# Feed-forward down products by tokens, bias and x1 added ahead on GpSimd, last attention chunk by tokens, end reordered

## Chip, cores and metric

The kernel runs on one core of one Trainium2 chip. The metric is device time in microseconds (us), the median of several executions; lower is better.

## The reference

One transformer layer with post-normalisation, batch 4, 1024 tokens, width 128, all in fp32. First a linear attention of 16 heads of 64:

```python
q, k, v = split(x @ W_qkv)                       # per head
q, k = relu(q @ W_f + b_f), relu(k @ W_f + b_f)
out = (q @ (k.T @ v)) / (q @ k.sum(tokens) + 1e-6)
x1 = layernorm(x + out @ W_out + b_out)
h = gelu(butterfly(x1 @ W_exp + b_exp, up_weights) + up_bias)   # 512 wide, exact gelu
y = butterfly(h, down_weights) @ W_con + b_con + down_bias
out = layernorm(x1 + y)
```

Both butterflies are linear, so the kernel folds each into one matrix, `wup` (128 x 512) and `wdn` (512 x 128), once at the start.

## The kernel before

Tokens are worked in 8 chunks of 512 (`n` = 0 to 7, `LAST` is 7). A hand-written schedule of 43 slots (`for s in range(SLOTS)`) is walked by TensorE (PE), ScalarE (ACT), VectorE (DVE) and GpSimd (POOL), each in its own program; tables such as `UPS`, `DOWN_SLOT` and `YT_SLOT` say in which slot a chunk's step stands, and semaphores join the engines. Every engine takes its instructions strictly in the written order. The keys' slots come first (0 to 27), then only queries, attention and feed-forward, then an end outside the slot loop for the last chunk, in two halves of 256 tokens (`g` = 0, 1).

One chunk goes so: DVE multiplies the queries by the reciprocals (`normalise_q`, L1179, tile `qn`), 8 pairs of heads a chunk; for the first three batches ACT and DVE split the product into a high and a low part (`qn_h`, `qn_l`), and PE adds three fast products per pair; in the last batch PE adds one plain fp32 product per pair (L686). The sum stands in bank `attn_ps` with features on the partitions. ACT copies it with the bias `b_out` into `attnT` (tile `late`), PE transposes it into the bank `desk` (L571), DVE adds x (`add_x`, L1204), takes statistics, GpSimd makes the reciprocal deviation (`rstd_of`, L522 and L525), and DVE normalises (`layer_norm_end`, L1197) to x1. PE transposes x1 into `desk`, ACT and DVE split it (`x1T_h`, `x1T_l`), PE makes four up products of three matmuls each into the three `ring` banks, ACT applies gelu into `hid` (L964).

`down(n)` (L732) then multiplies with `wdn` as stationary operand and `hid` as moving one, four matmuls of 128x512 that leave the result by features in a ring bank. `yT_copy` (ACT, L971) adds the bias into `yT` (tile `late`), `transpose_y` (PE, L571) turns it into `desk`, and `residual` (DVE, L1213) adds x1, followed by the second normalisation and the store. `desk` is one bank that many transposes share: each waits until its previous content has been taken (`take_desk`).

A plain fp32 matmul shows in the trace as two records, an fp32 transpose as one.

Of the kernel before, what the change touches and what calls it, by code (L numbers as in the profile page):

```python
# [5 lines left out]
def postln_linear_attention_butterfly_ffn_kernel(  # L6
# [106 lines left out]
    YT_SLOT = {}  # L113
    for n in range(ALLCH - 4):
        at = ATTN_LAST[n] + 3
        for i in range(HT):
            UPS[at + i] = [HT * n + i]
        DOWN_SLOT[at + HT] = n
        YT_SLOT[at + HT + 1] = n


    for n, ups, down, back in [(4, [33, 34, 35, 35], 36, 37), (5, [37, 37, 38, 38], 39, 42),
                               (6, [41, 41, 42, 42], None, None)]:
        for i in range(HT):
            UPS.setdefault(ups[i], []).append(HT * n + i)
        if n < LAST - 1:
            DOWN_SLOT[down] = n
            YT_SLOT[back] = n
# [13 lines left out]
    for s in range(SLOTS):  # L142
# [10 lines left out]
        if s in DOWN_SLOT:  # L153
            order.append(("down", DOWN_SLOT[s]))
# [3 lines left out]
    for use in [("down", LAST - 1), *[("up", HT * LAST + i, g) for g in range(2) for i in range(HT)],  # L158
                ("down", LAST, 0), ("down", LAST, 1)]:
        ring_of[use] = len(ring_of)  # L160
# [5 lines left out]
    for s in range(SLOTS):  # L166
# [5 lines left out]
        if s in YT_SLOT:  # L172
            order.append(("y", YT_SLOT[s]))
# [13 lines left out]
    for use in [("attn", LAST, 0), ("x1", LAST, 0), ("y", LAST - 1), ("y", LAST, 0)]:  # L187
        desk_of[use] = len(desk_of)
    spare_of = {("attn", LAST, 1): 0, ("x1", LAST, 1): 1, ("y", LAST, 1): 2}
# [5 lines left out]
    with ctx:  # L195
# [30 lines left out]
        bcon_col = sb("bcon_col", [128, 1])  # L226
        bdn_raw = sb("bdn_raw", [128, 1])
        bdn_col = sb("bdn_col", [128, 1])
# [24 lines left out]
        attnT, yT = late[:, 0, :], late[:, 1, :]  # L253
# [14 lines left out]
        coef_rows = sb("coef_rows", [HT, LOCAL, 256])  # L268
# [63 lines left out]
        s_smade = sem("spare_made")  # L332
        s_staken = sem("spare_taken")
# [34 lines left out]
        def half_bank(use):  # L368
            return desk if use[2] == 0 else spare_ps

        def half_made(use):

            return (s_dmade, desk_of[use] + 1) if use[2] == 0 else (s_smade, spare_of[use] + 1)

        def half_taken(use):
            return (s_dtaken, desk_of[use] + 1) if use[2] == 0 else (s_staken, spare_of[use] + 1)
# [4 lines left out]
        def _(sp):  # L381
# [47 lines left out]
            column(bcon_col[:, :], b_con)  # L429
            column(bdn_raw[:, :], down_bias)  # L430
# [40 lines left out]
            for n in range(1, LAST + 4):  # L471
                if n < ALLCH:
                    spread(n)
                if n >= 4:
                    store_out(n - 4)
# [8 lines left out]
        def _(pool):  # L484
# [34 lines left out]

            def rstd_of(i, n):  # L520
# [10 lines left out]
            for s in range(SLOTS):  # L531
                if s == WEIGHTS_SLOT:
                    pool.wait_ge(s_wuh, 1)
                    g.tensor_tensor(wup_l[:, :], y_up[:, :], wup_h[:, :].bitcast(fp32), ALU.subtract).then_inc(s_wul, 1)
                if s in ATT_T_SLOT:
                    rstd_of(0, ATT_T_SLOT[s])
                if s in YT_SLOT:
                    rstd_of(1, YT_SLOT[s])

# [11 lines left out]
            rstd_half(0, 1)  # L551
            rstd_of(1, LAST - 1)
# [4 lines left out]
        def _(pe):  # L557
# [117 lines left out]
            def add_attn(a):  # L675
# [6 lines left out]
                elif p == 0:  # L682
                    pe.wait_ge(s_atc, a // PAIRS)
                if a >= WHOLE:
# [24 lines left out]
            def transpose_y(n):  # L709
                take_desk(("y", n))  # L710
                pe.wait_ge(s_taken, ring_of["down", n] + 1)
                transpose_tiles(desk, lambda i: yT[:, i * 128:(i + 1) * 128]).then_inc(s_dmade, 1)

# [11 lines left out]

            def down(n):
                take_ring(("down", n))
                if n == 0:
                    pe.wait_ge(s_dtaken, desk_of["wdn",] + 1)
                for i in range(HT):  # L730
                    pe.wait_ge(s_taken, ring_of["up", HT * n + i] + 1)
                    last = t_.matmul(bank(("down", n))[:, :], wdn[:, i, :], hid[:, i, :],  # L732
                                     start=i == 0, stop=i == HT - 1)
                last.then_inc(s_made, 1)
# [27 lines left out]
            for s in range(SLOTS):  # L762
# [29 lines left out]
                if s in YT_SLOT:  # L792
                    transpose_y(YT_SLOT[s])
# [43 lines left out]
            def take_half(use):  # L837
                if use[2] == 0:
                    pe.wait_ge(s_dtaken, desk_of[use])
                elif spare_of[use]:  # L840
                    pe.wait_ge(s_staken, spare_of[use])
                else:

                    pe.wait_ge(s_dn, 3 * STAGES)

            def transpose_half(use, src):
                for i in range(2):
                    last = t_.transpose(half_bank(use)[:, i * 128:(i + 1) * 128], src(2 * use[2] + i), ident[:, :])
                last.then_inc(half_made(use)[0], 1)

            for g in range(2):
                take_half(("attn", LAST, g))
                pe.wait_ge(s_atc, LAST + 1 + g)
                transpose_half(("attn", LAST, g), lambda i: attnT[:, i * 128:(i + 1) * 128])
            down(LAST - 1)
            for g in range(2):
                take_half(("x1", LAST, g))
                pe.wait_ge(s_x1, LAST + 1 + g)
                transpose_half(("x1", LAST, g), lambda i: x1[:, LAST % X1BUF, i, :])
            for g in range(2):  # L860
# [9 lines left out]
                if g == 0:  # L870
                    transpose_y(LAST - 1)
            for g in range(2):
                use = ("down", LAST, g)
                take_ring(use)
                for i in range(HT):
                    pe.wait_ge(s_taken, ring_of["up", HT * LAST + i, g] + 1)
                    last = t_.matmul(bank(use)[:, 0:HALF], wdn[:, i, :], hid[:, i, g * HALF:(g + 1) * HALF],
                                     start=i == 0, stop=i == HT - 1)
                last.then_inc(s_made, 1)
            for g in range(2):  # L880
                take_half(("y", LAST, g))
                pe.wait_ge(s_taken, ring_of["down", LAST, g] + 1)
                transpose_half(("y", LAST, g), lambda i: yT[:, i * 128:(i + 1) * 128])

        @block.scalar
        def _(act):
# [72 lines left out]
            def gelu(f):  # L959
                n, i = f // HT, f % HT  # L960
                act.wait_ge(s_made, ring_of["up", f] + 1)
                if i == 0 and n:
                    act.wait_ge(s_made, ring_of["down", n - 1] + 1)
                a_.activation(hid[:, i, :], bank(("up", f))[:, :], ACT.Gelu, bias=bup_col[:, i:i + 1])\  # L964
                    .then_inc(s_taken, 1)

            def yT_copy(n):
                act.wait_ge(s_made, ring_of["down", n] + 1)
                if n:
                    act.wait_ge(s_dmade, desk_of["y", n - 1] + 1)  # L970
                a_.activation(yT[:, :], bank(("down", n))[:, :], ACT.Identity, bias=bdn_col[:, :]).then_inc(s_taken, 1)  # L971
# [18 lines left out]
            for s in range(SLOTS):  # L990
# [35 lines left out]
                if s in DOWN_SLOT:  # L1026
                    if s == min(DOWN_SLOT):
                        act.wait_ge(s_bc, 2)
                    yT_copy(DOWN_SLOT[s])
                for f in UPS.get(s, []):  # L1030
                    if f == 0:
                        act.wait_ge(s_bc, 2)
# [9 lines left out]
                if s == 5:  # L1042
                    act.wait_ge(s_bias, 16 * (3 + HT))
# [7 lines left out]
            act.wait_ge(s_at, PAIRS * ALLCH)  # L1051
            act.wait_ge(s_dmade, desk_of["attn", LAST - 1] + 1)
            for tok in halves:
                a_.activation(attnT[:, tok], attn_ps[:, tok], ACT.Identity, bias=bout_col[:, :]).then_inc(s_atc, 1)
            yT_copy(LAST - 1)
# [4 lines left out]
            act.wait_ge(s_made, ring_of["down", LAST - 1] + 1)  # L1060
            for g, tok in enumerate(halves):
                for i in range(HT):
# [4 lines left out]
            act.wait_ge(s_dmade, desk_of["y", LAST - 1] + 1)  # L1067
            for g, tok in enumerate(halves):
                use = ("down", LAST, g)
                act.wait_ge(s_made, ring_of[use] + 1)  # L1070
                a_.activation(yT[:, tok], bank(use)[:, 0:HALF], ACT.Identity, bias=bdn_col[:, :]).then_inc(s_taken, 1)

        @block.vector
        def _(dve):
# [126 lines left out]
            def add_x(n):  # L1201
                b, c = n // CHUNKS, n % CHUNKS
                dve.wait_ge(s_dmade, desk_of["attn", n] + 1)
                v.tensor_tensor(x1[:, n % X1BUF, :, :], desk[:, :].rearrange("p (t c) -> p t c", t=QUADS),  # L1204
# [4 lines left out]
            def residual(n):  # L1209
                dve.wait_ge(s_dmade, desk_of["y", n] + 1)  # L1210
                if n >= 2:
                    dve.wait_ge(s_out[n % 2], 16 * (n // 2))
                v.tensor_tensor(y[:, n % 2, :, :], desk[:, :].rearrange("p (t c) -> p t c", t=QUADS),  # L1213
                                x1[:, n % X1BUF, :, :], ALU.add).then_inc(s_dtaken, 1)
                dve.wait_ge(s_dtaken, desk_of["y", n] + 1)
# [29 lines left out]
            for s in range(SLOTS):  # L1245
# [30 lines left out]
                if s in YT_SLOT:  # L1276
                    residual(YT_SLOT[s])
# [7 lines left out]
                if s in YT_SLOT:  # L1285
                    layer_norm_end(1, YT_SLOT[s], y[:, YT_SLOT[s] % 2, :, :], s_yo)
# [18 lines left out]
                if s == WEIGHTS_SLOT:  # L1305
                    dve.wait_ge(s_bias, 16 * (3 + HT))
# [71 lines left out]
```

## Time and profile before

| | |
|---|---|
| median of 3 executions | 343.5 us (341.99 to 343.79) |
| the profiled execution, its own time | 344.24 us |
| its span in the trace | 342.4 us |
| PE busy | 321.1 us, 94% of the span |
| DVE busy | 229.2 us, 67% |
| ACT busy | 166.2 us, 49% |
| GpSimd busy | 81.9 us, 24%, nearly all of it before 80 us |
| mean granted PE clock | 0.997 of full speed |

Busy time of PE is the union of overlapping records, so start-to-start distances tell more of its pace than the length of one record. What is not in the span, 344.24 less 342.4, is 1.84 us.

### The profile page before, as it was taken

To read this page: it belongs to the slowest core of one execution; us is meant where nothing else is said; L and a number is where in the kernel's file an instruction comes from. 1 tells how busy PE (TensorE), PEld (TensorE's weight loads), DVE (VectorE), ACT (ScalarE), POOL (GpSimd) and SP (SyncE) were. 2 spreads that over 40 slices of the span, in tenths; PEclk is the share of its full clock that TensorE was granted. 3 is DMA by queue.
4 is the path that set the end of the run, shared out by engine and by line. 5 is a ranking of instruction groups with operands and counts; after the bars stand their busy time and mean duration, and the time that the engine had idled before them with its cause. 6 is when DMAs were issued, how large, how long until landed. Compare 5 with 4: busy or idle time off the path is not lost.

```text
span 342.4 us, 5147 instructions
## 1 busy us (share of the span) xinstructions
PE 321.1 (94%) x1845; PEld 224.2 (65%) x1845; DVE 229.2 (67%) x476; ACT 166.2 (49%) x280; POOL 81.9 (24%) x81
## 2 busy tenths in 40 slices
PE   5799899999999999999999999999999798989882
PEld 5666567767776776677767677577777566554462
DVE  3458999868698586857623876458637827477555
ACT  3533245435466454565474546365656543341451
POOL 4079999940000010101000110011001101111122
PEclk9999999999999999999999999999999999999998
DMA  6983143827406400900090006600380073740002
GB/s 185 281 273 134 71 174 124 299 77 182 125 2 144 107 0 6 235 11 3 8 228 15 0 2 144 138 0 3 77 202 2 3 191 90 164 127 18 24 9 62
DMA packets 25618, 33.75 MB, mean 99 GB/s; under 512 B 4184, under 2 KB 14456, under 8 KB 25592
## 3 DMA queue, kind: packets, MB, share of 16 engines
q1 hardware_dynamic: 25432, 33.38, 36.4%
q8 instruction: 15, 0.25, 0.3%
q14 instruction: 11, 0.09, 0.1%
q10 hardware_dynamic: 160, 0.03, 0.0%
HBM read 31.04 MB, written 2.36 MB: 98 GB/s over the span
## 4 chain that ended last, share of the span: by engine, by line
PE 72%; DVE 13%; DMA 5%; issue 4%; SPq 3%; POOL 2%; ACT 1%; POOLq 0%; DVEq 0%; ACTq 0%
PE ring L562 25%; PE kx_ps L636 12%; PE attn_ps L562 7%; PE ring L732 6%; PE ring L656 4%; PE attn_ps L686 4%; PE ring L616 3%; PE desk L571 3%; DMA bf_col<-in_L_attn_b_f_dram 2%; DVE qn L1179 2%; DMA x<-_L_ffn_down_weights_dram 2%; PE desk L670 2%; PE desk L645 2%; SPq L445 1%; DVE late L1096 1%
## 5 line engine op out<-in xcount | busy, mean ns | idle before, releaser
L908 ACT ACTIVATE q<-ring,bf_col 128x512 f32<-128x512 f32 x64 | 43.8, 688 | 52.1 <-PE ring L562 51.6
L522 POOL TENSOR_TENSOR var_eps<-mean_var,ln_eps 128x4 f32<-128x4 f32 x14 | 7.0, 503 | 223.8 <-DVE mean_var L1192 223.8
L636 PE MATMUL kx_ps<-k,xs 128*128 128x512 f32 x128 | 60.1, 592 | 0.0
L901 ACT ACTIVATE k<-ring 128x512 f32<-128x512 f32 x64 | 38.3, 598 | 28.3 <-PE ring L616 27.9
L1179 DVE TENSOR_TENSOR qn<-q,recips 128x512 f32<-128x512 f32 x64 | 42.3, 699 | 4.3 <-DMA recips<-recip_rows 4.3
L1078 DVE TENSOR_TENSOR qn_l<-qn,qn_h 128x512 fp32r<-128x512 f32 x48 | 32.2, 680 | 16.9 <-ACT qn_h L894 16.6
L514 POOL TENSOR_TENSOR y<-hid,y_up 128x512 f32<-128x512 f32 x18 | 35.4, 1986 | 15.3 <-DMA hid<-in_L_ffn_up_weights_dram 14.3
L894 ACT ACTIVATE qn_h<-qn 128x512 fp32r<-128x512 f32 x48 | 29.6, 627 | 14.8 <-DVE qn L1179 14.8
L562 PE MATMUL ring<-xT_h,wq_h 128*128 128x512 f32 x64 | 35.7, 558 | 0.0
L636 PEld LDWEIGHTS kx_ps<-k,xs 128*128 128x128 f32 x128 | 24.0, 189 | 17.8 <-issue 15.3
L1151 DVE TENSOR_TENSOR k_total<-k_total,k 128x1024 f32<-128x1024 f32 x24 | 34.4, 1432 | 0.9 <-ACT k L901 0.7
L562 PE MATMUL ring<-wk_h,xT_h 128*128 128x512 f32 x64 | 29.0, 453 | 0.0
L732 PE MATMUL ring<-hid,wdn 128*128 128x512 f32 x56 | 25.4, 596 | 0.0
L616 PE MATMUL ring<-bf_rows,ones_r 128*128 128x512 f32 x64 | 25.1, 393 | 0.1
L562 PE MATMUL ring<-xT_h,wq_l 128*128 128x512 f32 x64 | 25.2, 394 | 0.0
L562 PE MATMUL ring<-wk_h,xT_l 128*128 128x512 f32 x64 | 25.2, 394 | 0.0
L562 PE MATMUL ring<-xT_l,wq_h 128*128 128x512 f32 x64 | 25.1, 392 | 0.0
L562 PE MATMUL ring<-wk_l,xT_h 128*128 128x512 f32 x64 | 25.1, 392 | 0.0
L964 ACT ACTIVATE hid<-ring,bup_col 128x512 f32<-128x512 f32 x28 | 19.2, 686 | 10.5 <-PE ring L562 10.3
L562 PE MATMUL attn_ps<-qn_h,m_h 128*128 128x512 f32 x48 | 19.9, 415 | 1.1 <-DVE qn_l L1078 1.1
L562 PE MATMUL attn_ps<-qn_l,m_h 128*128 128x512 f32 x48 | 19.0, 395 | 0.0
L562 PE MATMUL attn_ps<-qn_h,m_l 128*128 128x512 f32 x48 | 18.8, 393 | 0.0
(159 smaller groups left out, 553.5 us busy)
## 6 DMA issues: line engine op xcount, KB each, us to landing
recips<-recip_rows SPq DMA_DIRECT2D x64, 256.0 KB, 5.2
hid<-in_L_ffn_up_weights_dram SPq DMA_DIRECT2D x9, 512.0 KB, 3.8
x<-_L_ffn_down_weights_dram SPq DMA_DIRECT2D x9, 512.0 KB, 4.4
xs<-in_L_attn_x_dram SPq DMA_DIRECT2D x4, 512.0 KB, 6.2
out_dram<-y SPq DMA_DIRECT2D x7, 256.0 KB, 3.7
q<-in_L_attn_W_qkv_dram SPq DMA_DIRECT2D x2, 512.0 KB, 9.0
q<-in_L_attn_W_qkv_dram SPq DMA_DIRECT2D x2, 256.0 KB, 3.1
q<-in_L_attn_W_out_dram SPq DMA_DIRECT2D x2, 256.0 KB, 8.7
```

The costliest lines, as they stand in the source:

```text
L514: g.tensor_tensor(term_up[f].rearrange("p (hi j lo) -> p hi j lo", j=2, lo=lo), w[:, :, :, :, f], yv[:, :, f:f + 1, :].to_broadcast([128, ...
L562: last = t_.matmul(dst, lhsT, rhs, start=start and n == 0, stop=stop and n == len(pairs) - 1)
L616: t_.matmul(dst, ones_r[:, :], bf_rows[:, :], start=False, stop=True).then_inc(s_made, 1)
L636: t_.matmul(kx_ps[half], xs[b % XBUF][:, t, :], k[kt % KRING][:, half * CH:(half + 1) * CH], start=t == 0, stop=t == TILES - 1).then_inc(s ...
L732: last = t_.matmul(bank(("down", n))[:, :], wdn[:, i, :], hid[:, i, :], start=i == 0, stop=i == HT - 1)
L894: a_.activation(dst, src, ACT.Copy).then_inc(done, 1)
L901: a_.activation(k[kt % KRING][:, half * CH:(half + 1) * CH], bank(("k", kt, half))[:, :], ACT.Relu).then_inc(s_taken, 1)
L908: a_.activation(q[:, i % QRING, :], bank(("q", i))[:, :], ACT.Relu, bias=bf_col[:, :])\
L964: a_.activation(hid[:, i, :], bank(("up", f))[:, :], ACT.Gelu, bias=bup_col[:, i:i + 1])\
L1078: v.tensor_tensor(dst, src, high.bitcast(fp32), ALU.subtract).then_inc(done, 1)
L1151: v.tensor_tensor(k_total[:, :], k_total[:, :], k[kt % KRING][:, :], ALU.add).then_inc(s_ks, 1)
L1179: v.tensor_tensor(qn[:, a % NRING, :], q[:, a % QRING, :], recips[:, a % PAIRS // RC, a % RC, :], ALU.mult).then_inc(s_qn, 1)
```

## The change

The down product is turned round: `hid` becomes the stationary operand and `wdn` the moving one, sixteen matmuls of 128x128 in four groups of 128 tokens (`down_group`), straight into the bank `spare_ps`, by tokens. The ACT copy and PE's transposes of y go away, and DVE's `residual` reads `spare_ps` directly. What `residual` added before, x1, and the bias are added ahead by GpSimd into `y` (`with_bias`, one addition of 128x512 a chunk, right behind the normalisation of x1). The biases come as rows, broadcast over the partitions by three DMAs that SP issues behind `spread(1)`; the two DMAs that loaded them as columns go.

The last chunk's attention is also made by tokens, four 128x128 matmuls a pair, so its copy and transposes go; GpSimd adds `b_out` to the last chunk of x in place, in slot 30. Chunk 6's four up products all stand in slot 42, behind the last attention sum. The end outside the loop is written in another order, and chunk 6's down product is split into its four groups between the last chunk's steps.

```diff
-                               (6, [41, 41, 42, 42], None, None)]:
+                               (6, [42, 42, 42, 42], None, None)]:
...
+            def with_bias(n, tiles, done):
+                pool.wait_ge(s_x1, done)
+                pool.wait_ge(s_brow, 1)
+                if n >= 2:
+                    pool.wait_ge(s_out[n % 2], 16 * (n // 2))
+                bias = bdn_row.rearrange("p (o c) -> p o c", o=1).to_broadcast([128, tiles.stop - tiles.start, C])
+                g.tensor_tensor(y[:, n % 2, tiles, :], x1[:, n % X1BUF, tiles, :], bias, ALU.add).then_inc(s_pre, 1)
...
-                if s in YT_SLOT:
-                    rstd_of(1, YT_SLOT[s])
+                if s in Y_SLOT:
+                    rstd_of(1, Y_SLOT[s])
+                if s in X1T_SLOT:
+                    with_bias(X1T_SLOT[s], slice(0, QUADS), X1T_SLOT[s] + 1)
+                if s == NO_KEYS + 2:
+                    pool.wait_ge(s_kxt, 2 * TILES * BATCH)
+                    last = xs[(BATCH - 1) % XBUF][:, (CHUNKS - 1) * QUADS:CHUNKS * QUADS, :]
+                    g.tensor_tensor(last, last, bout_row.rearrange("p (o c) -> p o c", o=1)
+                                    .to_broadcast([128, QUADS, C]), ALU.add).then_inc(s_xb, 1)
...
+            for h in range(2):
+                with_bias(LAST, slice(2 * h, 2 * h + 2), LAST + 1 + h)
             rstd_of(1, LAST - 1)
...
+                if a >= BATCH * STEPS - PAIRS:
+                    pe.wait_ge(s_qn, a + 1)
+                    for i in range(QUADS):
+                        tok = slice(i * 128, (i + 1) * 128)
+                        last = t_.matmul(attn_ps[:, tok], qn[:, a % NRING, tok], m_whole[:, p, :],
+                                         start=p == 0 and i == 0, stop=p == PAIRS - 1 and i == QUADS - 1)
...
+            def down_group(n, i, dst):
+                for j in range(HT):
...
+                    last = t_.matmul(dst, hid[:, j, i * 128:(i + 1) * 128], wdn[:, j, :],
+                                     start=j == 0, stop=j == HT - 1)
...
+            transpose_x1_half(0)
+            take_down(LAST - 1)
+            down_before_last(0)
+            transpose_x1_half(1)
+            down_before_last(1)
+            up_half(0)
+            down_before_last(2)
+            down_before_last(3)
+            up_half(1)
...
             def residual(n):
-                dve.wait_ge(s_dmade, desk_of["y", n] + 1)
...
+                dve.wait_ge(s_pre, n + 1)
...
+            layer_norm_half_end(0, 0, last_x1, s_x1)
+            layer_norm_end(1, LAST - 2, y[:, (LAST - 2) % 2, :, :], s_yo)
+            layer_norm_half_end(0, 1, last_x1, s_x1)
```

On PE, from slot 40 to the first up product of the last chunk, before:

```order
L686 MATMUL attn_ps<-qn,k_total 128x512 x2
L562 MATMUL ring<-x1T_h,wup_h 128x512
...
L686 MATMUL attn_ps<-qn,k_total 128x512
L571 MATMUL desk<-ident,late 128x128 x4
L686 MATMUL attn_ps<-qn,k_total 128x512
...
L848 MATMUL desk<-ident,late 128x128 x2
L848 MATMUL spare_ps<-ident,late 128x128 x2
L732 MATMUL ring<-hid,wdn 128x512 x4
L848 MATMUL desk<-ident,x 128x128 x2
L848 MATMUL spare_ps<-ident,x 128x128 x2
L562 MATMUL ring<-x1T_h,wup_h 128x256
```

The same stretch of the changed kernel, where L717 is the attention by tokens and L764 `down_group`:

```order
L717 MATMUL attn_ps<-k_total,qn 128x128 x16
L589 MATMUL ring<-x1T_h,wup_h 128x512
...
L888 MATMUL desk<-ident,x 128x128 x2
L764 MATMUL spare_ps<-wdn,hid 128x128 x4
L888 MATMUL attn_ps<-ident,x 128x128 x2
L764 MATMUL spare_ps<-wdn,hid 128x128 x4
L589 MATMUL ring<-x1T_h,wup_h 128x256
```

The last four attention sums now stand together ahead of chunk 6's up products; the transposes of attention and y are gone, and two groups of chunk 6's down product stand between the x1 transposes, ahead of the first up product.

On GpSimd, slots 30 to 32 of the changed kernel (before, the four rows of `var_eps` and `rstd` stood here alone):

```order
L536 TENSOR_TENSOR var_eps<-mean_var,ln_eps 128x4
L539 TENSOR_TENSOR rstd<-var_eps,minus_half 128x4
L562 TENSOR_TENSOR xs<-xs,rows 128x512
L536 TENSOR_TENSOR var_eps<-mean_var,ln_eps 128x4
L539 TENSOR_TENSOR rstd<-var_eps,minus_half 128x4
L532 TENSOR_TENSOR y<-x,rows 128x512
```

Two additions of 128x512 have come in, one behind the deviations of y (chunk 2), one behind those of x1 (chunk 4).

On DVE, the last chunk's first normalisation in the changed kernel; before, L1197 of y stood ahead of both additions, and the two pairs of L1329 of x together behind them:

```order
L1236 TENSOR_TENSOR y<-spare_ps,y 128x512
...
L1336 TENSOR_TENSOR x<-attn_ps,xs 128x256
...
L1336 TENSOR_TENSOR x<-attn_ps,xs 128x256
...
L1348 TENSOR_SCALAR x<-x,mean_var,rstd 128x128 x2
L1216 TENSOR_SCALAR y<-y,mean_var,rstd 128x128 x4
L1348 TENSOR_SCALAR x<-x,mean_var,rstd 128x128 x2
```

The normalisation of chunk 5's y (L1216) now stands between the two halves of x1.

## Rows read from the trace of the kernel before

**Rows 1.** The page: busy time by engine, and the chain that ended last.

```profile
PE 321.1 (94%) x1845; PEld 224.2 (65%) x1845; DVE 229.2 (67%) x476; ACT 166.2 (49%) x280; POOL 81.9 (24%) x81
...
PE 72%; DVE 13%; DMA 5%; issue 4%; SPq 3%; POOL 2%; ACT 1%; POOLq 0%; DVEq 0%; ACTq 0%
```

**Rows 2.** Timeline at one down product (start, length, engine, line, operation).

```profile
294.74 3.60 PE L732 MATMUL ring<-hid,wdn 128*128 128x512 f32 x8
...
298.18 0.60 PE L571 MATMUL desk<-ident,x 128*128 128x128 f32 x4
...
298.61 1.02 PE L686 MATMUL attn_ps<-qn,k_total 128*128 128x512 f32 x2
```

**Rows 3.** Timeline of PE at the start: plain fp32 128x128 matmuls.

```profile
5.61 1.96 PE L589 MATMUL attn_ps<-wf_diag,q 128*128 128x128 f32 x8
7.37 1.91 PE L589 MATMUL spare_ps<-wf_diag,q 128*128 128x128 f32 x8
...
15.94 1.06 PE L589 MATMUL spare_ps<-wf_diag,q 128*128 128x128 f32 x8
16.83 1.45 PE L636 MATMUL kx_ps<-k,xs 128*128 128x512 f32 x3
```

**Rows 4.** Timelines of DVE and of POOL around 130 and 137 us.

```profile
129.65 1.29 DVE L1179 TENSOR_TENSOR qn<-q,recips 128x512 f32<-128x512 f32 x2
137.47 2.38 DVE L1179 TENSOR_TENSOR qn<-q,recips 128x512 f32<-128x512 f32 x2
...
137.71 1.59 POOL L534 TENSOR_TENSOR wup_l<-y_up,wup_h 128x512 fp32r<-128x512 f32 x1 [9.12 <-ACT wup_h L894]
```

**Rows 5.** Timelines of DVE and PE, 255 to 290 us; in brackets the wait before.

```profile
261.71 1.12 DVE L1197 TENSOR_SCALAR y<-y,mean_var,rstd 128x128 f32<-128x128 f32 x4 [1.18 <-POOL rstd L525]
262.75 1.29 DVE L1179 TENSOR_TENSOR qn<-q,recips 128x512 f32<-128x512 f32 x2
...
269.53 1.28 DVE L1179 TENSOR_TENSOR qn<-q,recips 128x512 f32<-128x512 f32 x2
...
272.37 0.47 PE L562 MATMUL attn_ps<-qn_h,m_h 128*128 128x512 f32 x1 [0.59 <-DVE qn_l L1078]
...
274.68 1.09 PE L670 MATMUL desk<-vo,kx 128*64 128x128 f32 x16 [0.67 <-DVE x1T_l L1078]
```

**Rows 6.** Timelines of PE at three other waits for DVE.

```profile
195.42 0.66 PE L571 MATMUL desk<-ident,late 128*128 128x128 f32 x4 [0.62 <-DVE xT_l L1078]
...
300.33 0.66 PE L571 MATMUL desk<-ident,late 128*128 128x128 f32 x4 [0.69 <-DVE x1T_l L1078]
...
306.66 1.10 PE L686 MATMUL attn_ps<-qn,k_total 128*128 128x512 f32 x2 [0.31 <-DVE qn L1179]
```

**Rows 7.** Timeline and chain of the end, from 315 us.

```profile
315.92 0.68 DVE L1179 TENSOR_TENSOR qn<-q,recips 128x512 f32<-128x512 f32 x1
...
318.92 1.02 PE L686 MATMUL attn_ps<-qn,k_total 128*128 128x512 f32 x2
...
323.57 0.42 DVE L1316 TENSOR_TENSOR x<-desk,xs 128x256 f32<-128x256 f32 x1
...
328.38 1.85 PE ring L562 x12
...
330.66 1.55 PE ring L562 x12
...
330.70 0.69 DVE L1213 TENSOR_TENSOR y<-desk,x 128x512 f32<-128x512 f32 x1 [1.58 <-PE desk L571]
...
334.12 1.12 DVE L1197 TENSOR_SCALAR y<-y,mean_var,rstd 128x128 f32<-128x128 f32 x4 [1.40 <-POOL rstd L525]
...
336.00 0.42 DVE L1316 TENSOR_TENSOR y<-desk,x 128x256 f32<-128x256 f32 x1 [0.77 <-PE desk L848]
...
337.15 0.39 DVE L1316 TENSOR_TENSOR y<-spare_ps,x 128x256 f32<-128x256 f32 x1
```

**Rows 8.** DMA issues: count, KB each, median us to landing.

```profile
out_dram<-y SPq DMA_DIRECT2D x7, 256.0 KB, 3.7
```

More of the change, by code:

```diff
@@ L127, in postln_linear_attention_butterfly_ffn_kernel @@
             DOWN_SLOT[down] = n
-            YT_SLOT[back] = n
+            Y_SLOT[back] = n
     WEIGHTS_SLOT = 16
@@ L157, in postln_linear_attention_butterfly_ffn_kernel @@
             ring_of[use] = len(ring_of)
-    for use in [("down", LAST - 1), *[("up", HT * LAST + i, g) for g in range(2) for i in range(HT)],
-                ("down", LAST, 0), ("down", LAST, 1)]:
+    for use in [("up", HT * LAST + i, g) for g in range(2) for i in range(HT)]:
         ring_of[use] = len(ring_of)
@@ L252, in postln_linear_attention_butterfly_ffn_kernel @@
         late = sb("late", [128, 2, CH])
-        attnT, yT = late[:, 0, :], late[:, 1, :]
+        attnT = late[:, 0, :]
         x1 = sb("x1", [128, X1BUF, QUADS, C])
@@ L267, in postln_linear_attention_butterfly_ffn_kernel @@
         bias_rows = sb("bias_rows", [HT, 128])
-        coef_rows = sb("coef_rows", [HT, LOCAL, 256])
+        rows = sb("rows", [128, LOCAL * 256])
+        coef_rows = rows[0:HT, :].rearrange("p (s n) -> p s n", s=LOCAL)
+        bout_row, bdn_row, bcon_row = (rows[:, i * C:(i + 1) * C] for i in range(3))
         coef_cols = sb("coef_cols", [128, STAGES - LOCAL, 2, 4])
@@ L473, in _ @@
                     spread(n)
+                if n == 1:
+                    sp.wait_ge(s_br, 3 * LOCAL)
+                    for dst, src in [(bout_row, b_out), (bdn_row, down_bias), (bcon_row, b_con)]:
+                        sp.dma_start(dst, src.rearrange("(o n) -> o n", o=1).to_broadcast([128, C])).then_inc(s_rows, 16)
                 if n >= 4:
@@ L724, in up_tile, with take_down @@
                       (x1T_h[:, :], x1T_l[:, :])).then_inc(s_made, 1)
-            def down(n):
[L727 to L734, printed above, removed]
+            def down_group(n, i, dst):
+                for j in range(HT):
+                    if i % 2 == 0:
+                        use = ("up", HT * n + j, i // 2) if n == LAST else ("up", HT * n + j)
+                        pe.wait_ge(s_taken, ring_of[use] + 1)
+                    last = t_.matmul(dst, hid[:, j, i * 128:(i + 1) * 128], wdn[:, j, :],
+                                     start=j == 0, stop=j == HT - 1)
+                return last
+            def take_down(n):
+                if n == 0:
+                    pe.wait_ge(s_dn, 3 * STAGES)
+                    pe.wait_ge(s_dtaken, desk_of["wdn",] + 1)
+                else:
+                    pe.wait_ge(s_dnt, n)
+            def down(n):
+                take_down(n)
+                for i in range(QUADS):
+                    last = down_group(n, i, spare_ps[:, i * 128:(i + 1) * 128])
+                last.then_inc(s_down, 1)
             def bias_columns():
@@ L835, in _, with transpose_x1_half, up_half @@
                     transpose_x1(X1T_SLOT[s])
[L837 to L846, printed above, removed]
+            def transpose_x1_half(g):
+                use = ("x1", LAST, g)
+                if g == 0:
+                    take_desk(use)
+                pe.wait_ge(s_x1, LAST + 1 + g)
                 for i in range(2):
-                    last = t_.transpose(half_bank(use)[:, i * 128:(i + 1) * 128], src(2 * use[2] + i), ident[:, :])
+                    last = t_.transpose(half_bank(use)[:, i * 128:(i + 1) * 128], x1[:, LAST % X1BUF, 2 * g + i, :],
+                                        ident[:, :])
                 last.then_inc(half_made(use)[0], 1)
[L851 to L860, printed above, removed]
+            def up_half(g):
                 for i in range(HT):
@@ L869, in _, with down_before_last @@
                           (x1T_h[:, tok], x1T_l[:, tok])).then_inc(s_made, 1)
-                if g == 0:
-                    transpose_y(LAST - 1)
-            for g in range(2):
[L873 to L883, printed above, removed]
+            def down_before_last(i):
+                down_group(LAST - 1, i, spare_ps[:, i * 128:(i + 1) * 128]).then_inc(s_dgrp, 1)
+            transpose_x1_half(0)
[7 more added lines that the diff above has]
+            up_half(1)
+            for g in range(2):
+                use = ("y", LAST, g)
+                pe.wait_ge(*half_taken(("x1", LAST, g)))
+                for i in range(2):
+                    last = down_group(LAST, 2 * g + i, half_bank(use)[:, i * 128:(i + 1) * 128])
+                last.then_inc(half_made(use)[0], 1)
         @block.scalar
@@ L962, in gelu @@
                 if i == 0 and n:
-                    act.wait_ge(s_made, ring_of["down", n - 1] + 1)
+                    act.wait_ge(s_down, n)
                 a_.activation(hid[:, i, :], bank(("up", f))[:, :], ACT.Gelu, bias=bup_col[:, i:i + 1])\
                     .then_inc(s_taken, 1)
[L967 to L971, printed above, removed]
             act.wait_ge(s_wT, 1)
@@ L1059, in _ @@
                 hi(x1T_h[:, tok], half_bank(("x1", LAST, g))[:, 0:HALF], s_x1h)
-            act.wait_ge(s_made, ring_of["down", LAST - 1] + 1)
             for g, tok in enumerate(halves):
+                act.wait_ge(s_dgrp, 2 * g + 2)
                 for i in range(HT):
@@ L1066, in _ @@
                         .then_inc(s_taken, 1)
[L1067 to L1071, printed above, removed]
         @block.vector
@@ L1275, in _ @@
                     add_x(ATT_T_SLOT[s])
-                if s in YT_SLOT:
-                    residual(YT_SLOT[s])
+                if s in Y_SLOT:
+                    residual(Y_SLOT[s])
                 for a in split_spreads(s)[1:]:
```

114 lines of the change are left out of this document (54 added, 60 removed).

## The prediction

> **What bounds the kernel now.** I read the page first: PE is busy for 94% of the span and makes up 72% of the chain that ended last, DVE 13% [rows 1]. So time that goes from PE's program counts, except where PE waits for another engine. The second view is PE's timeline, for its pace and its waits. The third is DVE's timeline over the stretches where PE waits for DVE: from 261 to 276 us DVE pauses only for GpSimd's deviations (the 1.18 in the row at 261.71), and PE waits for it, 0.59 and 0.67 us in the two rows shown [rows 5], and shorter cases stand at 195, 300 and 306 us [rows 6]. The last is the end from 316 us, where PE, DVE and GpSimd hand single steps to each other.
>
> **Down product, by tokens.** Before: eight records from 294.74 to 298.18, 3.44 us, 0.43 a record [rows 2]. After: sixteen matmuls, 32 records. The trace has plain fp32 matmuls of just this shape, each with its own stationary load. Eight of them take 16.83 - 15.94 = 0.89 us, 0.111 each; earlier, eight took 7.37 - 5.61 = 1.76 us, 0.22 each [rows 3]. I take 0.111, since it is from an already running PE, as every down product is; 0.22 is the other bound. So 32 x 0.111 = 3.56 us, 0.12 more per chunk, six times inside the slot loop: +0.7 us. The last chunk's eight attention sums go from 0.86 to 0.89 each: +0.2.
>
> **Transposes of y removed.** Four transposes cost 298.61 - 298.18 = 0.43 us of PE [rows 2] (a like group; y's have the same shape). Five stand in PE's stream before the end, chunks 0 to 4. Chunk 0's is followed by PE waiting 0.62 us for DVE at 195.42, which only grows: 0 gained. Chunk 2's opens the stretch where DVE is late: 0. Chunks 1 and 3 give 0.43 each. Chunk 4's waited another 0.69 us for `desk` at 300.33 [rows 6]; of the 1.12 us, I let the wait for DVE's `qn` at 306.66, which grows as PE comes earlier, take back a third: -0.75. Together -1.6 us. ACT's copies were hidden behind PE and are worth nothing by themselves.
>
> **GpSimd's additions.** Two DVE products of 128x512, both inputs in SBUF, take 1.29 us at 129.65, but 2.38 us at 137.47, when GpSimd's addition of 128x512 (1.59 us) runs beside them: +1.1 us [rows 4]. `with_bias` is such an addition, and starts just when DVE goes from normalising x1 to the same pair of products. So each costs DVE up to 1.1 us, with 0 as the lower bound. For chunks 0, 1, 2, 3 and 5 DVE then has idle time or PE is still behind: cover, so 0 (1.1 each if the cover is gone). For chunk 4 it meets the pair at 269.53, with PE already waiting for DVE behind it [rows 5]: +1.1. The addition to x in slot 30 starts as GpSimd ends the deviations, at 261.7, beside the normalisation at 261.71 and the pair at 262.75 [rows 5]. No row shows a normalisation beside such an addition. If it is spared, a third of the 1.6 us is left for the pair, 0.4; if not, 1.1; I take the middle, +0.7. For chunk 6 see the end.
>
> The Trainium skill (GPSIMD Engine Reference, Key points) says GpSimd shares its SBUF interfaces with VectorE, with contention for instructions "in a 2-port perf mode or with two SBUF inputs". The trace agrees on the second kind, by the 2.38 us; no row shows the first kind. By that rule the slot-30 addition would cost its full 1.1 and my sum would end 0.4 us later. The page's advice to give elementwise work to VectorE speaks against the change as well.
>
> **The middle together:** +0.7 + 0.2 - 1.6 + 1.1 + 0.7 = +1.1 us by 316 us. The up products now leave the ring a bank earlier, and SP's three broadcasts of rows fall into a stretch where SP waits; both 0.
>
> **The end**, on before's time scale. `with_bias` of chunk 6 delays DVE's last products, which had 0.4 us of slack, so the one at 315.92 ends at 317.3 in place of 316.6. The last attention sum no longer waits behind two up products and a transpose: it ends near 318.3, against 318.92 + 1.02 = 319.94. DVE needs no transpose of y: `residual(5)` runs 317.3 to 319.3 (2.0 us: the 334.12 + 1.12 - 330.70 = 4.54 of a whole normalisation less the normalising 1.12 and the wait 1.40) [rows 7]. The last chunk's x1 addition then starts at 319.35, against 323.57.
>
> What follows is two programs. DVE: half 0 and half 1 at 1.15 each (336.00 to 337.15) until 321.65; GpSimd first has chunk 5's deviations (1.4) and then half 0's (a pair of shorter operations, I estimate 1.0 from that 1.4) to 321.7; normalising half 0 takes 0.6 (half of 1.12), chunk 5 takes 1.12, half 1 takes 0.6: 324.1. PE from there: transposes 0.4, a down group 0.9, up half 1.6 (1.85 and 1.55 in the rows), two groups 1.8, up half 1.6, the last two halves 1.8 each: 334.0. DVE: `residual(6)` can start behind the fourth group, 324.1 + 0.4 + 0.9 + 1.6 + 1.8 = 328.8, plus 0.2 to see it, and takes 4.54 to 333.55; half 0 then 1.15, and half 1 starts at 334.75. DVE is the later by a little. Before, that addition started at 337.15 [rows 7]; all behind it is unchanged. The end gives 337.15 - 334.75 = -2.4 us.
>
> GpSimd's two `with_bias` halves of the last chunk wait for the store of chunk 5, which lands 3.7 us [rows 8] after 323.5, at 327.2; two operations of at most 0.8 (half of 1.59) end at 328.8, ahead of `rstd_of(1, 6)` at 331. That costs 0; behind them stand those deviations, and a store that lands 2 us late would delay the end by about that.
>
> **Sum:** +1.1 - 2.4 = -1.3 us: 344.24 - 1.3 = 342.9 for an execution like the profiled one, which lies 0.7 above the median of the runs. Against the median: 343.5 - 1.3 = 342.2 us.
>
> **Rivals.**
> - *The additions are absorbed* (faster). If GpSimd's slowing of DVE reaches PE nowhere, 1.1 + 0.7 go from the middle and 0.55 from the end: -3.65, 339.9 us. For it: DVE has idle time around most chunks. Against: the 2.38 us row, and PE's waits right behind the pair at 269.53.
> - *DVE's lost time reaches PE in most chunks* (slower). Eight additions at 1.1 are 8.8 us; my sum holds 2.35 of it. Once more than 1.3 us beyond that reaches PE, the kernel is slower. If half of the remaining 6.4 does: +1.9, 345.4 us. For it: DVE runs near PE's pace also at 185 to 196 us. Against: PE waits for DVE there only once, 0.62 us.
> - *Small matmuls run at 0.22 us a record.* 3.6 us more for each of six down products, and 0.9 for each of eight attention sums and some 7 us at the end: over 30 us, 375. For it: the rows at 5.61; against: those at 15.94.
> - *The end is not shorter, since DVE's chain replaces PE's*: -2.4 shrinks to 0 and the middle's +1.1 stays, 344.6 us. Against: the 4 us earlier start of the x1 addition follows from removed steps alone.
>
> **Chances.** Forecast 0.45 (its own range 341.0 to 343.5), absorbed 0.32, DVE reaching PE 0.12, small matmuls 0.03, end not shorter 0.08. The range to hold 8 in 10 goes from the absorbed case with a little below it, 339.4, to the end-not-shorter case, 344.7. A measurement tells about 0.5%, 1.7 us, from no change, so faster means below 341.8. A third of the forecast's share and nearly all of the absorbed case lie there: 0.45. Slower means above 345.2: the small matmuls and most of DVE's case, 0.13. The rest, 0.42, is within 0.5%.
>
> **What would show it.** Down records 0.11 us apart, a down product of 3.5 to 3.7 us; `with_bias` at 1.3 to 2.1 us with the DVE pair beside it at 2.3 to 2.4; PE's waits near 267 to 276 us grown by 1 to 2 us in total; the last chunk's x1 addition 3 to 4 us earlier relative to the end of DVE's last product; the last half's addition some 5.2 us before the span's end as now. The prediction is wrong if those waits did not grow, if new waits of PE for `qn_l` stand in the keys' slots, or if the down products take 5 us or more.

## The result, and the profile after

| | before | after |
|---|---|---|
| median | 343.64 us (4 runs beside it) | 355.08 us (354.17 to 356.53, 4 runs) |
| profiled execution, its span | 344.24, 342.4 us | 354.17, 352.3 us |
| mean granted PE clock | 0.997 | 0.981 |

The ratio is 1.034, with an interval of 1.030 to 1.038: 11.4 us slower, where 342.2 was forecast and 344.7 was the upper end of the range. The page of the changed kernel, busy time and chain (for [rows 1]):

```profile
PE 321.5 (91%) x2041; PEld 242.2 (69%) x2041; DVE 232.1 (66%) x475; ACT 159.4 (45%) x269; POOL 95.4 (27%) x92
...
PE 63%; DVE 13%; DMA 8%; issue 5%; SPq 5%; POOL 4%; ACT 1%; POOLq 0%; DVEq 0%; ACTq 0%
```

PE has no more to do than before (321.1), but its share of the chain fell from 72% to 63%, and DMA, SP's queue and GpSimd rose from 10% together to 17%. So the lost time is waiting. The view of waits says where (total, times, longest):

```profile
POOL y L532 <- DMA out_dram<-y: 78.8, 5, 20.7
...
DVE y L1216 <- POOL rstd L539: 19.8, 6, 8.0
...
PE attn_ps L717 <- DVE qn L1198: 7.3, 1, 7.3
```

`with_bias` (L532) waits five times for a store of `out`, up to 20.7 us; behind two of these waits DVE's normalisation of y waits up to 8.0 us for GpSimd's deviations (longest before: 1.4); behind that PE waits 7.3 us. The timelines of SP, GpSimd, DVE and PE show the same stretch (start, length, in brackets the wait before):

```profile
273.44 1.70 SPq L438 DMA_DIRECT2D recip_rows<-recip  x4
276.19 5.13 SPq L446 DMA_DIRECT2D recips<-recip_rows  x8
281.36 0.60 SPq L452 DMA_DIRECT2D out_dram<-y  x1
293.79 1.71 SPq L438 DMA_DIRECT2D recip_rows<-recip  x4
296.53 12.93 SPq L446 DMA_DIRECT2D recips<-recip_rows  x8
309.50 36.78 SPq L452 DMA_DIRECT2D out_dram<-y  x4
```

```profile
256.95 1.30 POOL L532 TENSOR_TENSOR y<-x,rows 128x512 f32<-128x512 f32 x1 [20.75 <-DMA out_dram<-y]
260.81 0.56 POOL L536 TENSOR_TENSOR var_eps<-mean_var,ln_eps 128x4 f32<-128x4 f32 x1 [2.55 <-DVE mean_var L1211]
...
288.62 1.27 POOL L532 TENSOR_TENSOR y<-x,rows 128x512 f32<-128x512 f32 x1 [18.42 <-DMA out_dram<-y]
...
313.63 1.26 POOL L532 TENSOR_TENSOR y<-x,rows 128x512 f32<-128x512 f32 x1 [16.28 <-DMA out_dram<-y]
```

```profile
291.19 1.11 DVE L1216 TENSOR_SCALAR y<-y,mean_var,rstd 128x128 f32<-128x128 f32 x4 [6.85 <-POOL rstd L539]
...
316.19 1.11 DVE L1216 TENSOR_SCALAR y<-y,mean_var,rstd 128x128 f32<-128x128 f32 x4 [7.98 <-POOL rstd L539]
```

```profile
294.36 1.91 PE L697 MATMUL desk<-vo,kx 128*64 128x128 f32 x16 [2.32 <-DVE x L1225]
...
300.18 3.73 PE L764 MATMUL spare_ps<-wdn,hid 128*128 128x128 f32 x32
303.75 0.60 PE L598 MATMUL desk<-ident,x 128*128 128x128 f32 x4
...
318.05 2.05 PE L717 MATMUL attn_ps<-k_total,qn 128*128 128x128 f32 x8 [7.25 <-DVE qn L1198]
```

The longest of the five waits held up no deviations: the addition of chunk 3 ran at 256.95, and GpSimd then still stood 2.55 us until DVE had the input of the next deviations ready. What decides is whether deviations fall due while the addition stands, and that happened twice, at 291 and at 316 us. Both stalls are in the chain that ended last (start, length, what):

```profile
281.36 7.10 DMA out_dram<-y
...
307.63 0.59 DVE qn L1198
...
308.85 0.61 SPq L446
...
309.50 3.97 DMA out_dram<-y
...
313.63 1.26 POOL y L532
...
315.13 1.03 POOL rstd L539
```

The second stall reads as a circle from DVE over SP's queue, the DMA and GpSimd back to DVE. SP issues its DMAs in written order, and the store of chunk n-4 stands behind `spread(n)`, eight broadcasts of the reciprocals, the last of which may only go when DVE has used up the old ones (`qn`, 308.22). Only then is chunk 3's store issued (309.50). `with_bias(5)`, which GpSimd comes to at 297.4 and whose x1 is normalised by 298.5, writes the half of `y` that this store reads and so stands until 313.6. The deviations of chunk 4's y stand behind it in GpSimd's queue, though DVE had their input ready at 307.6. At 316.2 DVE goes on.

The first stall has the same order of SP's queue and of GpSimd's, but another length. Chunk 2's y was normalised at 264.6; its store stands behind `spread(6)`, which SP could begin only at 273.44, when the new reciprocals were made, and whose eight broadcasts go out without a further wait. Issued at 281.36, directly behind them, the store took 7.10 us to land, where 3.7 is the median before [rows 8]. `with_bias(4)` waited for it until 288.62, and chunk 3's deviations behind that.

With 1.19 us as the usual wait (1.18 in [rows 5]), the two stalls cost DVE 6.85 - 1.19 + 7.98 - 1.19 = 12.45 us.

### The profile page after: what moved, and what is told of

It is laid out like the page before. It is cut to its first block, busy times and chain, and to the rows that moved or that the text cites. A ratio compares the mean times of both kernels' runs of the same rounds, so it can differ in the third digit from the quotient of the medians.

```text
span 352.3 us, 5536 instructions
## 1 busy us (share of the span) xinstructions
PE 321.5 (91%) x2041; PEld 242.2 (69%) x2041; DVE 232.1 (66%) x475; ACT 159.4 (45%) x269; POOL 95.4 (27%) x92
## 4 chain that ended last, share of the span: by engine, by line
PE 63%; DVE 13%; DMA 8%; issue 5%; SPq 5%; POOL 4%; ACT 1%; POOLq 0%; DVEq 0%; ACTq 0%
PE ring L589 22%; PE kx_ps L663 12%; PE attn_ps L589 7%; PE spare_ps L764 6%; PE ring L643 3%; PE ring L683 3%; DMA out_dram<-y 3%; SPq L446 3%; PE desk L598 3%; DMA x<-_L_ffn_down_weights_dram 2%; DVE qn L1198 2%; POOL rstd L539 2%; PE desk L697 2%; PE desk L672 2%; DMA bf_col<-in_L_attn_b_f_dram 2%
## 5 line engine op out<-in xcount | busy, mean ns | idle before, releaser
L1097 DVE TENSOR_TENSOR qn_l<-qn,qn_h 128x512 fp32r<-128x512 f32 x48 | 33.2, 703 | 16.6 <-ACT qn_h L932 16.2
L1170 DVE TENSOR_TENSOR k_total<-k_total,k 128x1024 f32<-128x1024 f32 x24 | 35.7, 1486 | 0.7 <-ACT k L939 0.5
L532 POOL TENSOR_TENSOR y<-x,rows 128x512 f32<-128x512 f32 (+1 forms) x9 | 12.9, 1443 | 81.4 <-DMA out_dram<-y 78.8
L764 PE MATMUL spare_ps<-wdn,hid 128*128 128x128 f32 x224 | 26.7, 276 | 0.0
L764 PEld LDWEIGHTS spare_ps<-wdn,hid 128*128 128x128 f32 x224 | 25.9, 192 | 1.0 <-issue 0.8
L1216 DVE TENSOR_SCALAR y<-y,mean_var,rstd 128x128 f32<-128x128 f32 x28 | 8.8, 375 | 19.8 <-POOL rstd L539 19.8
```

Source lines behind the costliest of these rows:

```text
L764: last = t_.matmul(dst, hid[:, j, i * 128:(i + 1) * 128], wdn[:, j, :], start=j == 0, stop=j == HT - 1)
L1097: v.tensor_tensor(dst, src, high.bitcast(fp32), ALU.subtract).then_inc(done, 1)
L1170: v.tensor_tensor(k_total[:, :], k_total[:, :], k[kt % KRING][:, :], ALU.add).then_inc(s_ks, 1)
```

## The experiments

Medians are against 343.5 us for the kernel before in each group of runs (343.54, 343.35 and 343.48). The changed kernel was not run again in these groups: differences from its 355.08 us are between groups, whose medians before lie within 0.3 us of each other. Theory 1: GpSimd's queue stands behind a store that is issued late. Theory 2: the additions slow DVE through a shared interface. Theory 3: the small matmuls or the new end cost the time.

**The store first.** SP's loop issues the store ahead of the spread:

```diff
             for n in range(1, LAST + 4):
+                if n >= 4:
+                    store_out(n - 4)
                 if n < ALLCH:
                     spread(n)
...
-                if n >= 4:
-                    store_out(n - 4)
```

> Change against the changed kernel: in SP's program the store of chunk n-4 stands ahead of the reciprocals' DMAs of chunk n, not behind them. Theory 1 (GpSimd's addition waits for a store that SP issues late, and the deviations queued behind it hold up VectorE): the two waits for deviations of 6.85 and 7.98 us shrink to the usual 1.2, the kernel loses about 12 of its 355 us and comes to 342 to 344. Theory 2 (the shared memory interface of GpSimd and VectorE costs the time) and theory 3 (small matmuls and a reordered end cost it): the order of SP's queue changes neither, 353 to 355 us.

Measured: 341.78 us, ratio 0.9954 (0.9926 to 0.9981), so 13.3 us come back and the kernel is a little faster than before. Waits and SP's timeline in it:

```profile
POOL y L532 <- DVE x L1216: 7.4, 6, 1.2
DVE y L1216 <- POOL rstd L539: 7.4, 6, 1.4
...
POOL y L532 <- DMA out_dram<-y: 3.5, 1, 3.5
```

```profile
263.83 0.40 SPq L452 DMA_DIRECT2D out_dram<-y  x1
272.70 1.70 SPq L438 DMA_DIRECT2D recip_rows<-recip  x4
275.43 5.14 SPq L446 DMA_DIRECT2D recips<-recip_rows  x8
285.87 0.40 SPq L452 DMA_DIRECT2D out_dram<-y  x1
```

The stores go out ahead of the spreads, the additions never wait for one inside the loop, and DVE's wait for the deviations is the usual one. The stores also land sooner: in this trace none of them takes more than 2.8 us. Nothing of the additions, the matmuls or the end was touched, so theories 2 and 3 are not the cause of the 11.4 us.

**Control: the same edit on the kernel before.**

> The kernel before with the same edit of SP's queue as in the first run, a control. Theory 1: no engine waits there for a store, so 343 to 344 us, no difference. A rival, that an earlier store is a gain by itself (less traffic beside the loads of the reciprocals), would give 341 to 342.

343.18 us, 0.9994 (0.9969 to 1.002). SP's order by itself is worth nothing; it matters only once an engine with a queue behind it waits for the store.

**One store first.** The store goes ahead of the spread only for n = 7, which frees `with_bias(5)` alone.

> The changed kernel with only one store issued ahead of its spread, that of chunk 3 (for n = 7), which with_bias(5) waits for. If each blocked addition costs its own wait, only the wait at 316 us (7.98 us against a usual 1.19) goes and the one at 291 us (6.85) stays: 355.1 - 6.8 = 348.3 us. If the delays were one common cause (chunk 4's late start carried on to chunk 5's), either nothing comes back (355) or all of it (342).

347.34 us, 1.0096 (1.0059 to 1.0132). DVE's wait at 309 is 1.19 again, the one at 291 stays at 6.79. One of the two stalls is removed, and 7.7 us of the loss come back, where that stall was 6.79 and 6.8 was expected; so the two stalls are separate, and each costs its own time.

**The additions late.** SP as in the changed kernel; each addition stands directly ahead of the deviations of its own chunk's y:

```diff
                 if s in Y_SLOT:
+                    with_bias(Y_SLOT[s], slice(0, QUADS), Y_SLOT[s] + 1)
                     rstd_of(1, Y_SLOT[s])
-                if s in X1T_SLOT:
-                    with_bias(X1T_SLOT[s], slice(0, QUADS), X1T_SLOT[s] + 1)
```

> Change against the changed kernel: each addition with the bias stands on GpSimd directly ahead of the deviations of the same chunk's y, some five slots later, so that no other chunk's deviations are queued behind its wait for a store; SP's queue is as in the changed kernel. Theory 1: it is what stands behind the wait that costs, so 342 to 345 us, as with the store issued earlier. Theory 2: the additions still collide with VectorE's work, 352 to 355. Theory 3: 355, no change.

343.82 us, 1.0012 (0.9991 to 1.0034): inside the loop the stores are no longer waited for, and 11.3 us come back. It stays 2 us behind the version with the store first. The traces suggest why, though no run tests it. Each addition now starts 0.06 us ahead of DVE's normalisation of x1 (GpSimd and DVE, this version):

```profile
270.30 1.27 POOL L532 TENSOR_TENSOR y<-x,rows 128x512 f32<-128x512 f32 x1
```

```profile
270.36 2.06 DVE L1216 TENSOR_SCALAR x<-x,mean_var,rstd 128x128 f32<-128x128 f32 x4 [1.19 <-POOL rstd L539]
```

The normalisation takes 2.06 in place of 1.12 us, and five others of x1 and one of y at 323.56 likewise (2.05 to 2.08). Chunk 3's y is normalised at 286.74 here and at 284.73 with the store first, 2.0 us apart, of which 0.94 came in at 270.36.

**No additions on GpSimd.** DVE adds x1 itself; the biases `b_con` and `down_bias`, and the last chunk's `b_out`, are left out.

> Change against the changed kernel: GpSimd's additions (bias and x1, and the one to x in slot 30) are left out, and VectorE adds x1 itself, as before the change; the biases b_con, down_bias and, for the last chunk, b_out are left out of the result. Theory 1: the waits for the store are gone with the additions, 340 to 342 us, the first run less the collisions of one or two us. Theory 2: about the same, 340 to 342, while the first run stays at 353. Theory 3: 353 to 355.

340.94 us, 0.9923 (0.9896 to 0.995). That is 0.8 us under the version with the store first, with intervals that overlap: all of GpSimd's additions together cost about this much once no queue stands behind a store.

**The up products as before.** Store first, and `UPS` of chunk 6 back to `[41, 41, 42, 42]`.

> The version with the store ahead of the spread, and chunk 6's up products back in slots 41, 41, 42, 42. If putting the last attention sums ahead of two up products is what gives the end part of its gain, the last sum comes some 1.7 us later and so does the x1 addition of the last chunk: up to 1.7 us slower than that version, 343.4 us. If the end is bound by DVE's products and by PE's total work alone, the time does not move: 341.8 us.

342.87 us, 0.9984 (0.9955 to 1.0012). The medians of the two versions differ by 1.1 us, but their intervals overlap; the traces settle it. DVE here:

```profile
320.10 0.42 DVE L1336 TENSOR_TENSOR x<-attn_ps,xs 128x256 f32<-128x256 f32 x1 [1.12 <-PE attn_ps L717]
...
335.04 0.39 DVE L1336 TENSOR_TENSOR y<-attn_ps,y 128x256 f32<-128x256 f32 x1
```

From the same point, DVE's last product (316.38 here, 316.36 with the last sums first), the last chunk's x1 addition waits 1.12 us for the last attention sum, and the last half's addition is at 335.04 against 333.93. The reorder is worth 1.1 us of the end.

**The addition to x moved.** Store first, and `b_out` added to x in slot 32 in place of 30, behind `with_bias(4)`.

> The version with the store ahead of the spread, and the addition of b_out to x moved from slot 30 to slot 32, behind with_bias(4), where DVE is not normalising. If a GpSimd addition that starts together with a normalisation is what doubles it (1.12 to 2.06 us at 262), and PE stands behind DVE there, the normalisation goes back to 1.12 and about 0.9 us comes back: 340.8 us. If the additions cost PE nothing in that stretch (DVE has slack), no change: 341.8 us. If the addition now meets DVE's subtractions instead, DVE loses 0.5 to 1 us there and the time stays at 341.8 or rises to 342.5.

342.3 us, 0.9955 (0.9921 to 0.9989): no gain. The collision moved with the addition. Store first (first fence) and this version (second), DVE:

```profile
261.73 2.08 DVE L1216 TENSOR_SCALAR y<-y,mean_var,rstd 128x128 f32<-128x128 f32 x4 [1.19 <-POOL rstd L539]
...
272.58 1.53 DVE L1097 TENSOR_TENSOR qn_l<-qn,qn_h 128x512 fp32r<-128x512 f32 x2
```

```profile
262.52 1.12 DVE L1216 TENSOR_SCALAR y<-y,mean_var,rstd 128x128 f32<-128x128 f32 x4 [1.19 <-POOL rstd L539]
...
272.41 2.61 DVE L1097 TENSOR_TENSOR qn_l<-qn,qn_h 128x512 fp32r<-128x512 f32 x2
```

0.96 us were won at the normalisation and 1.08 lost at the pair of subtractions.

**The addition to x in DVE's idle time,** with it left out and the store-first version repeated beside it:

```diff
-                if s == NO_KEYS + 2:
+                if s == NO_KEYS + 4:
                     pool.wait_ge(s_kxt, 2 * TILES * BATCH)
+                    pool.wait_ge(s_qnl, WHOLE)
```

> Store ahead of the spread, and the addition of b_out to x in slot 32, started only when DVE has made the last low part of the queries, at about 277 us, where DVE then waits 3.2 us for a DMA and GpSimd has nothing to do until 283. If what the two earlier places cost is only that the addition met DVE's work in the stretch where PE stands behind DVE, the normalisation stays at 1.12 us, the pair of subtractions at 1.53, and 0.9 us comes back against the version with the addition in slot 30: 340.9 us. If PE does not stand behind DVE there, 341.8 us.

> Store ahead of the spread, and the addition of b_out to the last chunk of x left out (the last chunk is without b_out). The bound for the version before: 340.9 us if the collision is the whole cost of this addition, 341.8 us if it costs nothing.

> The version with the store ahead of the spread once more, beside the two others on the same chip, so that less than a microsecond can be told: 341.8 us, 0.9 us above both if the collision at 262 us reaches PE.

340.57 us, 0.9919 (0.9888 to 0.9951), with the addition in idle time; 340.78, 0.9921 (0.9893 to 0.9949), without it (last chunk without `b_out`); 341.85, 0.9949 (0.9925 to 0.9973), for the repeat. GpSimd and DVE of the first:

```profile
276.66 1.27 POOL L563 TENSOR_TENSOR xs<-xs,rows 128x512 f32<-128x512 f32 x1 [4.30 <-DVE qn_l L1098]
```

```profile
280.05 0.69 DVE L1199 TENSOR_TENSOR qn<-q,recips 128x512 f32<-128x512 f32 x1 [3.53 <-DMA recips<-recip_rows]
```

In the 3.53 us in which DVE waits for a DMA the addition is free: the medians of the version with it and of the one without it are alike, and both lie 1.1 to 1.3 us under the repeat. The intervals overlap, so the size rests on the traces. There the collision at 262 us reaches PE by way of ACT, which splits DVE's late products before it frees a ring bank. PE's next query product, with the store first and then with the addition in idle time:

```profile
266.30 0.50 PE L589 MATMUL ring<-xT_h,wq_h 128*128 128x512 f32 x1 [1.21 <-ACT hid L1002]
```

```profile
265.70 0.51 PE L590 MATMUL ring<-xT_h,wq_h 128*128 128x512 f32 x1 [0.24 <-ACT hid L1003]
```

The wait is 0.97 us shorter, as much as the normalisation's 0.96; in the repeat it is 1.20 and without the addition 0.24. This version is the fastest complete one: 2.9 us under the kernel before and 14.5 under the change as made.

## Why the prediction was wrong

**The step that failed** is the price of `with_bias`: "So each costs DVE up to 1.1 us, with 0 as the lower bound." That priced the operation and its collision with DVE, and not its wait. The diff shown in the change has the line, `pool.wait_ge(s_out[n % 2], 16 * (n // 2))`. I did follow it, for the last chunk alone: "That costs 0; behind them stand those deviations, and a store that lands 2 us late would delay the end by about that." That sentence is the mechanism, applied to the wrong chunk. Before, the same wait stood in DVE's `residual(n)`, reached only when chunk n's down product and its transpose were done (319.12 us for chunk 5). The change moved it to the normalisation of x1, which for chunk 5 ended at 293.53 + 1.12 = 294.65 before. The buffer is asked for some 24 us sooner, while the instruction that frees it kept its place in SP's queue. The addition for chunk 5, in which I saw only a collision covered by idle time ("cover, so 0"), and that for chunk 4, priced at +1.1, cost DVE 6.79 and 5.66 us of waiting. Of the added wait I named neither what is late in SP's queue nor what is queued behind it on GpSimd, so no rival had this case, and the 344.7 of the range held none of it. The second stall was to be read from the code and the timeline of before. Chunk 3's store is issued there at 304.92; with the 3.7 us of [rows 8] and the 2.56 us from the start of the addition to DVE (313.63 to 316.19), DVE could go on at 311.2, and the trace has it normalise chunk 4's y at 304.80. That estimate gives a stall of 6.4 us against 6.79 measured. The first was harder to see: the same sum from the store at 279.61 ends at 285.9, ahead of the normalisation at 286.43, since the median hides how long a store behind eight broadcasts takes.

**The small matmuls: right.** A down product takes 303.75 - 300.18 = 3.57 us, 0.111 a record, against 3.56 forecast. Their rival at 0.22 fell. The granted clock is 1.00 in the rows at 5.61 that it came from, so the clock does not explain them; why they are slow stays open.

**The contention, right in kind, wrong in place.** The operation of [rows 4] is GpSimd's subtraction for `wup_l`, of the same size as the additions. I charged 1.1 us for `with_bias(4)` beside the pair of products; with the store first that pair starts first and stays at 1.29 us, and the addition is the slow one (2.27). So one of my signs of being wrong was there: PE's four waits for DVE from 267 to 276 us did not grow as forecast (2.42 us in total before, 2.44 in the changed kernel, 2.74 with the store first). The slot-30 addition I charged at 0.7; it costs DVE 0.96. Together 1.8 forecast; the rival's list has the sum of GpSimd's additions at 2.35 with 0.55 for chunk 6 (the working of the end has 0.7 there), and leaving all of them out gives back 0.8. Store first, the middle costs +0.2 us where +1.1 was forecast: the normalisation of chunk 6's x1 is at 312.20 against 312.00 before.

**The end: right in kind, its gain half as large again as forecast.** From the last product of DVE to the last half's addition, before took 337.15 - 315.92 = 21.23 us [rows 7]. The changed kernel, and the store-first one:

```profile
329.37 0.68 DVE L1198 TENSOR_TENSOR qn<-q,recips 128x512 f32<-128x512 f32 x1
...
346.94 0.39 DVE L1336 TENSOR_TENSOR y<-attn_ps,y 128x256 f32<-128x256 f32 x1
```

```profile
316.36 0.68 DVE L1198 TENSOR_TENSOR qn<-q,recips 128x512 f32<-128x512 f32 x1
...
333.93 0.39 DVE L1336 TENSOR_TENSOR y<-attn_ps,y 128x256 f32<-128x256 f32 x1
```

Both 17.57 us, 3.66 less. The forecast of -2.4 held a delay of 0.7 by chunk 6's addition that did not come (the last three products before it stay at 1.89 us); without it, it was 3.1. The last chunk's x1 addition starts 318.88 - 317.04 = 1.84 us behind the end of DVE's last product, against 6.97 before and 319.35 - 317.3 = 2.05 in the forecast. GpSimd's additions for the last chunk waited 3.5 us for the store, hidden behind PE, as predicted.

So what was priced at +1.1 - 2.4 = -1.3 us came, store first, to +0.44 (DVE's last product at 316.36 against 315.92) - 3.66 = -3.2 us between two profiled executions, and -1.8 between the medians. Both terms came out more favourable than forecast, so that the medians come within 0.5 us of the forecast is partly luck.

The 11.4 us are one kind of wait that was not priced. The 13.3 us that came back are 0.85 more than the two stalls' 12.45, but the stalls are not simply what came back. Followed along DVE, the changed kernel lies behind the store-first one by these amounts. By 262.5 us it is 0.76 late: the addition that had stood until 256.95 met a subtraction, which took 1.82 in place of 0.69 us.

```profile
256.98 1.82 DVE L1097 TENSOR_TENSOR qn_l<-qn,qn_h 128x512 fp32r<-128x512 f32 x1 [1.12 <-ACT qn_h L932]
```

The first stall adds 5.66; between the stalls 2.0 is made up, as the store-first version has a wait of 3.14 for ACT there (289.58) that the changed kernel has not; the second stall adds 6.79, and 1.3 more follows directly behind it. DVE's wait for the next transposes, in the changed kernel and with the store first:

```profile
320.98 0.69 DVE L1225 TENSOR_TENSOR x<-desk,xs 128x512 f32<-128x512 f32 x1 [1.88 <-PE desk L598]
```

```profile
308.43 0.69 DVE L1225 TENSOR_TENSOR x<-desk,xs 128x512 f32<-128x512 f32 x1 [0.55 <-PE desk L598]
```

Behind it stands PE's granted clock, the first number behind the five engines of each row (changed kernel behind its second stall, then store first):

```profile
318.00:320.00 2.00, 1.95 (x9) 1.98 (x10) 1.10 (x2) 0.00 (x0) 0.00 (x0) 0.50 0.47 139
```

```profile
300.00:316.00 16.00, 15.53 (x102) 12.44 (x101) 11.72 (x38) 4.58 (x7) 5.74 (x5) 1.00 0.30 72
```

After its wait of 7.25 us PE takes 319.88 - 318.05 = 1.83 us for eight records at the lower of its two clock levels, 1.2 GHz against 2.4; with the store first the same eight take 307.79 - 306.83 = 0.96. With the last 0.5 us, ahead of DVE's last product, the sum is 329.37 - 316.36 = 13.0 us, between spans that differ by 13.1. So the wait of PE cost more here than its length.

## What to carry to other kernels

When work moves to an emptier engine, move its waits on paper too: for each semaphore, when is it now asked for, which queue signals it, behind what does the signal stand there, and which urgent small operation stands behind the waiting one. An idle share (GpSimd is busy for 24%; 55.4 of its 81.9 us lie before 80 us, 26.5 behind) says nothing of that. If a buffer is asked for sooner, the DMA that frees it has to be issued sooner, and ahead of a bulk of other transfers where it can be; here that is two lines in SP's loop and 13 us.

## What the runs showed of the hardware

Of two operations of GpSimd and DVE that collided, the one that started first kept its time and the other lost most of the time that they shared. An addition that started 0.06 us ahead of the normalisation (270.30 and 270.36): 1.27 and 2.06 us, 0.94 lost of the 1.21 shared. A pair of products that started 0.17 us ahead of the addition (270.52 and 270.69, store first): 1.29 and 2.27 us, 1.00 lost of 1.12. Three products ahead (295.55 and 295.72): 1.89 and 2.85, 1.58 lost of 1.72. DVE and GpSimd in the store-first version:

```profile
270.52 1.29 DVE L1198 TENSOR_TENSOR qn<-q,recips 128x512 f32<-128x512 f32 x2
```

```profile
270.69 2.27 POOL L532 TENSOR_TENSOR y<-x,rows 128x512 f32<-128x512 f32 x1 [1.23 <-DVE x L1216]
```

The Trainium skill (SBUF — State Buffer, Who interferes with whom) says that issue order, not op shape, decides who blocks, and that the other blocks fully. These rows agree on the order; of the block they show four fifths and more. The same section of the Trainium skill says that `tensor_scalar` can contend. The trace agrees: the normalisation is one, with one tensor input in SBUF.

An addition that starts a little further behind the first of several DVE operations seems to get in between them, and delays what follows: at 0.24 us the pair takes 2.38 ([rows 4], GpSimd's operation 1.59), at 0.34 the subtractions at 272.41 take 2.61 (GpSimd's 1.72), at 0.37 the four operations of the normalisation at 323.56, additions late, take 2.06 (GpSimd's 1.34). At 0.17 us it waited for both. No run here shows where between 0.17 and 0.24 that turns.

A store of 256 KB issued directly behind eight broadcasts of 256 KB took 7.10 us to land (281.36); with the stores ahead of the broadcasts none took more than 2.8. That may come from the transfers ahead of it; no run here separates this from the rest.
